# One core, blockwise FP4 feed-forward: the last group of tiles is exchanged throughout and takes its residual from a second copy of x

## The reference

```
w = weights[conditions]                      # one 64 x 64 matrix per sample
y = einsum('bct,bcd->bdt', x, w)             # mix the 64 channels of a sample
a = quant_dequant_mxfp4(y)                   # blocks of 32 along t: shared power-of-two scale,
W = quant_dequant_mxfp4(weight)              # values rounded to the FP4 grid
out = x + (a @ W.T + bias)                   # W is 512 x 512
```

## Time and profile before

| | us |
|---|---|
| runs | 97.59, 98.38, 98.47 |
| median | 98.38 |
| the profiled execution | 97.9 |
| its span, first to last instruction | 96.2 |
| PE busy / DVE busy / ACT busy | 84.4 / 81.9 / 75.3 |
| DMA moved | 22.17 MB, mean 230 GB/s |

### The profile page before, as it was taken

The page is one execution under the profiler, slowest core; times in us unless marked ns, Lnnn a source line. Parts: engine busy times, 40 slices in busy tenths (PEclk is TensorE's granted clock), DMA queues, the critical chain, the costliest instruction groups (busy, mean ns, idle before and its releaser), DMA issues.

```text
span 96.2 us, 2263 instructions
## 1 busy us (share of the span) xinstructions
PE 84.4 (88%) x715; PEld 41.2 (43%) x715; DVE 81.9 (85%) x138; ACT 75.3 (78%) x85; POOL 32.9 (34%) x60
## 2 busy tenths in 40 slices
PE   5999594999799998999899899989999989989800
PEld 4966252595482324344233433333352333445300
DVE  1248999999999999999999999999979999885600
ACT  4740498699998869999999999999999849957000
POOL 4273758399647548303000300320040021054000
PEclk9999999999999999999999999999999999999995
DMA  1898789694896789799999991896579399486992
GB/s 34 288 316 295 244 249 301 212 352 125 181 317 218 274 248 269 242 312 265 254 310 298 311 212 49 272 245 116 218 185 224 114 263 222 88 272 175 270 285 92
DMA packets 13901, 22.17 MB, mean 230 GB/s; under 512 B 4034, under 2 KB 4802, under 8 KB 13890
## 3 DMA queue, kind: packets, MB, share of 16 engines
q1 hardware_dynamic: 11456, 17.31, 56.4%
q0 software_dynamic: 2432, 4.73, 23.6%
q10 hardware_dynamic: 2, 0.00, 0.0%
HBM read 10.49 MB, written 8.39 MB: 196 GB/s over the span
## 4 chain that ended last, share of the span: by engine, by line
PE 44%; ACT 11%; DVE 10%; issue 6%; ACTq 0%; DVEq 0%
PE o_ps L357 20%; PE y_ps L357 5%; PE y_ps L306 5%; ACT y_sb L471 5%; ACT o_sb L493 4%; PE o_ps L352 4%; PE o_ps L337 3%; DVE a L654 3%; DVE n_int L625 2%; DVE top L645 2%; ACT z L463 1%; PE o_ps L382 1%; PE y_ps L367 1%; PE y_ps L300 1%; PE y_ps L318 1%
## 5 line engine op out<-in xcount | busy, mean ns | idle before, releaser
L357 PE MATMUL o_ps<-wT,aT 128*128 128x512 bf16 x100 | 23.8, 380 | 0.4 <-ACT aT L508 0.4
L183 POOL DMA_DIRECT2D mix<-in_L_cond_weights_dram x32 | 17.9, 560 | 12.4 <-issue 11.0
L625 DVE TENSOR_TENSOR n_int<-y_sb,inv 128x1024 int16<-128x1024 f32 (+1 forms) x17 | 19.5, 1155 | 0.2
L306 PE MATMUL y_ps<-x_sb,mix 64*64 64x512 f32 x120 | 15.6, 606 | 3.9 <-DMA mix<-in_L_cond_weights_dram 2.4
L272 POOL DMA_DIRECT2D x_sb<-o_sb x6 | 6.1, 1014 | 35.1 <-ACT o_sb L493 35.1
L382 PE MATMUL o_ps<-idle 128*128 128x128 bf16 x214 | 16.6, 235 | 1.2 <-DVE idle L664 1.2
L463 ACT ACTIVATE z<-y_ps 128x1024 bf16<-128x1024 bf16 x16 | 16.2, 1039 | 1.5 <-PE y_ps L306 1.2
L471 ACT COPY y_sb<-y_ps 128x1024 f32<-128x1024 f32 x16 | 16.3, 1035 | 0.0
L382 PEld LDWEIGHTS o_ps<-idle 128*128 128x128 bf16 x214 | 13.6, 105 | 5.1 <-issue 4.7
L480 ACT ACTIVATE zone<-inv 128x1024 int16<-128x1024 int16 (+2 forms) x11 | 11.6, 1074 | 3.8 <-DVE inv L618 3.8
L502 ACT COPY aT<-o_ps 128x1024 bf16<-128x1024 bf16 x14 | 13.7, 1045 | 1.0 <-PE o_ps L337 1.0
(11 more groups left out here) (52 smaller groups left out, 76.0 us busy)
## 6 DMA issues: line engine op xcount, KB each, us to landing
x_sb<-in_x_dram SPq DMA_DIRECT2D x7, 1024.0 KB, 6.4
out_dram<-x_sb SPq DMA_DIRECT2D x15, 256.0 KB, 3.6
x_sb<-o_sb POOLq DMA_DIRECT2D x6, 512.0 KB, 5.2
out_dram<-x_sb SPq DMA_DIRECT2D x6, 512.0 KB, 3.1
w_sb<-in_L_ffn_weight_dram SPq DMA_DIRECT2D x4, 256.0 KB, 3.4
x_sb<-in_x_dram SPq DMA_DIRECT2D x2, 512.0 KB, 6.6
out_dram<-x_sb POOLq DMA_DIRECT2D x4, 256.0 KB, 3.6
mix<-in_L_cond_weights_dram POOLq DMA_DIRECT2D x32, 16.0 KB, 4.5
```

Of the source, the lines that this page charges most:

```text
L183: queue.dma_start(mix[HALVES[i % 2], first + i // 2, :], table[bass.ds(row, 1), :, :].rearrange("o c d -> (o c) d")).then_inc(mix_in[step] ...
L306: last = nc.tensor.matmul(y_ps[HALVES[g], 2 * q + r, :], mix[HALVES[r], (step - 1) * GROUP + n, :], x_tiles(step, n)[HALVES[r], :], start= ...
L357: last = nc.tensor.matmul(o_bank(step, t), aT[:, t, c, :], wT[:, c, :], start=False, stop=(c == KC - 1))
L625: nc.vector.tensor_tensor(columns(n_int, t, n), columns(y_sb[:, step % 2, :, :], t, n), columns(inv, t, n), ALU.mult).then_inc(n_done, 1)
```

## The change

- The last group is mixed exchanged in both pairs (the straight form of `mix_pair` is gone), and its output tiles stay exchanged, with its transposes done one tile at a time on TensorE. Its residual therefore has to be exchanged as well: a second copy of the last group's x, `last_x`, is loaded by SP with four DMAs of 256 KB, and VectorE adds from it. The four tiles are stored by SP straight from `last_x` (three whole, the last in two halves). In DRAM such a tile is two runs of 64 rows, 256 KB apart.
- Group 7 is rescaled and turned in two pairs. Only its pair 0 gets its residual on TensorE. Tile 2 goes over `o_sb` and an accumulating DMA of POOL, tile 3 is added by VectorE. POOL takes over the store of group 6's pair 1.
- The first x is issued by ACT after its second `z_w`, not by SP ahead of the mixes. W is scaled, zoned and rounded in two pairs. TensorE's filler products (`keep_busy`) and the order of turning W and mixing group 2 move.
- `load_mixes` no longer tests the row numbers (the eight small instructions go).

Names and numbers: `after(step)` = step + 2, `late_part(part)` = 9 + part.

```diff
+        last_x = sb("last_x", [P, GROUP, T], F32)
...
+        exchanged_x_dram = x.rearrange("(s q g r) c t -> s q g r c t", q=2, g=2, r=2)
...
         def t_pair(step, q):
 
             if step < LAST - 1:
-                bank = 2 + q
-            else:
-                bank = 2 - q
-            return o_ps[:, bank, :].bitcast(BF16)
+                return o_ps[:, 2 + q, :].bitcast(BF16)
+            return y_ps[:, 3 - q, :].bitcast(BF16)
...
+                skip_runtime_bounds_check_because="cond holds row numbers of the table")
...
-            for h in range(2):
-                sp.dma_start(x_tiles(1, 2 * h, 2).rearrange("p (n t) -> p n t", n=2),
-                             x_dram[:, 2 * h:2 * h + 2, :]).then_inc(x_first_in[h], 16)
...
+            for t in range(GROUP):
+                sp.dma_start(last_x[:, t, :],
+                             exchanged_x_dram[LAST - 1, t // 2, :, t % 2, :, :]).then_inc(last_x_in, 16)
...
-                sp.wait_ge(x_added[step % 2], 16 * ((step + 1) // 2))
-                store(step, SUMMED, GROUP - SUMMED)
+                if step < LAST - 2:
+                    sp.wait_ge(x_added[step % 2], 16 * ((step + 1) // 2))
+                    store(step, SUMMED, GROUP - SUMMED)
+            sp.wait_ge(added, 1)
+            store(LAST - 1, GROUP - 1)
             for t in range(GROUP - 1):
-                sp.wait_ge(added, t + 1)
-                store(LAST, t)
+                sp.wait_ge(added, t + 2)
+                sp.dma_start(exchanged_dram[LAST - 1, t // 2, :, t % 2, :, :],
+                             last_x[:, t, :]).then_inc(stored, 16)
             for half in range(2):
-                sp.wait_ge(added, GROUP + half)
-                sp.dma_start(out_dram[:, TILES - 1, n_half(half)], x_tiles(LAST, GROUP - 1)[:, n_half(half)]
+                sp.wait_ge(added, GROUP + 1 + half)
+                sp.dma_start(exchanged_dram[LAST - 1, 1, :, 1, :, n_half(half)],
+                             last_x[:, GROUP - 1, n_half(half)]
                              ).then_inc(stored, 16)
-            sp.wait_ge(stored, 16 * (3 * (LAST - 2) + GROUP + 1))
-            sp.wait_ge(late_stored, 16 * 2 * 2)
+            sp.wait_ge(stored, 16 * (3 * (LAST - 2) - 1 + 1 + GROUP + 1))
+            sp.wait_ge(late_stored, 16 * 4)
...
+            pool.wait_ge(late_copied, 2)
+            for g in range(2):
+                pool.dma_start(exchanged_dram[LAST - 2, 0, g, :, :, :].rearrange("r c t -> c r t"),
+                               x_tiles(LAST - 1, 0, 2)[HALVES[g], :].rearrange("p (r t) -> p r t", r=2)
+                               ).then_inc(late_stored, 16)
+            pool.wait_ge(late_tile, 1)
+            pool.dma_start(x_tiles(LAST - 1, SUMMED), o_sb[:, (LAST - 1) % 2, 0, :], accum_op=ALU.add
+                           ).then_inc(x_added[(LAST - 1) % 2], 16)
+            pool.wait_ge(x_added[(LAST - 2) % 2], 16 * ((LAST - 1) // 2))
+            n0 = (LAST - 3) * GROUP + SUMMED
+            pool.dma_start(out_dram[:, n0:n0 + 2, :], x_tiles(LAST - 2, SUMMED, 2).rearrange("p (n t) -> p n t", n=2)
+                           ).then_inc(late_stored, 16)
+            pool.wait_ge(x_added[(LAST - 1) % 2], 16 * (LAST // 2))
+            n0 = (LAST - 2) * GROUP + SUMMED
+            pool.dma_start(out_dram[:, n0, :], x_tiles(LAST - 1, SUMMED)).then_inc(late_stored, 16)
...
-                if step == LAST and q == 1:
-
-                    for n in (2 * q, 2 * q + 1):
-                        for half in HALVES:
-                            last = nc.tensor.matmul(y_ps[half, n, :], mix[half, (step - 1) * GROUP + n, :],
-                                                    x_tiles(step, n)[half, :], start=True, stop=True)
-                        last.then_inc(y_ready, 1)
-                    return
...
             pe.wait_ge(y_copied, tiles_done(LAST, 3))
-            residual_pair(LAST - 1, 1)
-            for t in range(GROUP):
+            pe.wait_ge(a2_done, late_part(0))
+            turn_pair(LAST - 1, 0, straight=True)
+            residual_pair(LAST - 1, 0)
+            for t in range(2):
                 bias_tile(LAST - 1, t, start=False)
-
+            pe.wait_ge(a2_done, late_part(1))
+            turn_pair(LAST - 1, 1)
+            for t in range(2):
+                ffn_tile(LAST - 1, t)
+
+            pe.wait_ge(aT_ready, tiles_done(LAST - 1, 3))
+            for t in range(2, GROUP):
+                bias_tile(LAST - 1, t)
+            for t in range(2, GROUP):
+                ffn_tile(LAST - 1, t)
+
+            pe.wait_ge(pair_copied, 2 * (LAST - 2))
             bias_tile(LAST, 0)
...
+            def copy_late_tile():
+
+                act.wait_ge(x_added[(LAST - 1) % 2], 16 * ((LAST - 2) // 2))
+                act.wait_ge(o_ready, tiles_done(LAST - 1, SUMMED))
+                nc.scalar.copy(o_sb[:, (LAST - 1) % 2, 0, :], o_bank(LAST - 1, SUMMED)).then_inc(late_tile, 1)
...
-            for t in range(GROUP):
+            for t in range(2):
                 z_w(t)
-            zone_group(0)
+
+            for h in range(2):
+                act.dma_start(x_tiles(1, 2 * h, 2).rearrange("p (n t) -> p n t", n=2),
+                              x_dram[:, 2 * h:2 * h + 2, :]).then_inc(x_first_in[h], 16)
+            for t in range(2, GROUP):
+                z_w(t)
+            for q in range(2):
...
+            dve.wait_ge(last_x_in, 16 * GROUP)
             for t in range(GROUP - 1):
-                add_residual(LAST, t)
+                dve.wait_ge(o_ready, tiles_done(LAST, t))
+                nc.vector.tensor_tensor(last_x[:, t, :], o_bank(LAST, t), last_x[:, t, :], ALU.add).then_inc(added, 1)
             for half in range(2):
                 dve.wait_ge(o_ready, tiles_done(LAST, GROUP - 1) + half)
-                part = x_tiles(LAST, GROUP - 1)[:, n_half(half)]
-                nc.vector.tensor_tensor(part, last_half(half), part, ALU.add
-                                        ).then_inc(added, 1)
+                part = last_x[:, GROUP - 1, n_half(half)]
+                nc.vector.tensor_tensor(part, last_half(half), part, ALU.add).then_inc(added, 1)
```

More of the change, by code:

```diff
@@ L149, in tiles_done, with after, late_part @@
             return GROUP * (step - 1) + t + 1
+        def after(step):
+            return step + 2
+        def late_part(part):
+            return after(LAST - 1) + part
         def n_half(half):
@@ L180, in load_mixes @@
             _, rows = nc.values_load_multi_w_load_instructions(
-                cond_sb[:, 2 * first:2 * (first + len(tiles))], engines=[engine], min_val=0, max_val=S - 1)
+                cond_sb[:, 2 * first:2 * (first + len(tiles))], engines=[engine], min_val=0, max_val=S - 1,
+                skip_runtime_bounds_check_because="cond holds row numbers of the table")
             for i, row in enumerate(rows):
@@ L392, in _ @@
                 mix_pair(2, q)
-            pe.wait_ge(ident_ready, 1)
-            for q in range(2):
-                pe.wait_ge(a2_done, q + 1)
-                turn_pair(0, q, straight=True)
-            keep_busy(60)
+            keep_busy(48)
             mix_pair(3, 0)
-            for step in range(1, LAST):
+            for step in range(1, LAST - 1):
                 if step == 2:
@@ L415, in _ @@
                     residual_pair(step, 0)
-                pe.wait_ge(a2_done, step + 2)
+                pe.wait_ge(a2_done, after(step))
                 for q in range(2):
-                    turn_pair(step, q, straight=(q == 0 or step == LAST - 1))
+                    turn_pair(step, q, straight=(q == 0))
                 if step == 1:
@@ L459, in z_pair @@
                 if q == 0 and step > 1:
-                    act.wait_ge(z_used, step - 1)
+                    act.wait_ge(z_used, after(step - 2))
                 act.wait_ge(y_ready, tiles_done(step, 2 * q + 1))
@@ L623, in round_y @@
                 if t == 0:
[L624 removed]
+                    dve.wait_ge(inv_done, after(step))
                 nc.vector.tensor_tensor(columns(n_int, t, n), columns(y_sb[:, step % 2, :, :], t, n),
@@ new lines, in _ @@
+            other_zones(LAST - 1)
+            tree_2(LAST + 4)
+            limit(LAST - 1, after(LAST - 1), 0, 2)
+            tree_3(LAST + 4)
+            rescale(LAST - 1, late_part(0), 2 * LAST, 0, 2)
+            block_max(LAST + 2)
+            limit(LAST - 1, after(LAST - 1), 2, 2)
+            lowest_zone(LAST + 2)
+            rescale(LAST - 1, late_part(1), 2 * LAST, 2, 2)
+            lift(LAST, LAST + 2)
+            top_zone(LAST + 2)
+            invert(LAST + 2)
+            round_y(LAST, 0, 1)
@@ new lines, in _ @@
+            limit(LAST, after(LAST), 0, 1)
+            for t in range(1, GROUP):
+                round_y(LAST, t, 1)
+                rescale(LAST, late_part(1 + t), 2 * LAST + t, t - 1, 1)
+                limit(LAST, after(LAST) + t, t, 1)
+            rescale(LAST, late_part(1 + GROUP), 2 * LAST + GROUP, GROUP - 1, 1)
```

(3 more changed lines are left out.)

249 lines of the change are left out of this document (121 added, 128 removed).

## The result

| | before | changed |
|---|---|---|
| median of 4 runs, us | 98.25 | **122.48** |
| lowest and highest | 97.59, 98.47 | 122.18, 122.61 |
| span of the profiled execution | 96.2 | 120.9 |
| ratio, with its 95% interval | | **1.2476** [1.2409, 1.2543] |

The change costs 24.2 us; 118.3 was forecast, in a range of 110 to 127, and slower had a chance of 0.84. The time is inside the range, 4.2 above the forecast.

The account below looks back on a forecast made before the run. PE, DVE and ACT bound the middle in step; the last group's transfers on two engines would set the end. Lower-end span 110.2 plus 6.4 standing over gives 116.6; with 1.7 outside the span, 118.3 us, range 110 to 127.

Parts of the forecast that it names:

- Two engines: `last_x` loads and stores, first dimension 2, all run on the same 2 engines; 21.1 us for each megabyte; chance 0.81.
- The rate: Each DMA engine moves 24.8 GB/s, so the last group's 512 KB on each of two engines takes 21.1 us.
- what stands over on the two engines: Work left at 86 us from the `last_x` loads: between 0 and 12.8 us, half of it, 6.4, taken.
- an empty queue: Lower end at the last stores: nothing queues, data moves from 89.1 us, plus 21.1 gives a span of 110.2.
- other loads move forward: If other loads leave the stretch from 34 to 86 us earlier, 0 us stands over; if none does, 12.8.
- The bound of engines that never rest: Upper end: the two engines work without pause from 2.3 us on, span 119.3, or 129.7 at the slower rate.
- SP's stall: Rival: two engines, and SP's issue stalls behind full queues, delaying middle and last stores; 120 to 127; no separate chance.
- Compute: Compute ends 1.7 us earlier: 2.2 gained in the last groups, 0.5 lost at the start; last addition near 89.8.
- first maximum: Sign at the start: group 1's first maximum starts near 15.5 us, against 15.21 before.
- The 0.5 us at the start: Handling W in pairs, with ACT's two zones ahead of group 1's z: 0.5 us lost, between 1.3 gained and 1.2 lost.
- Sixteen engines: Rival: `last_x` transfers spread over all sixteen engines, last store leaves 1.7 us earlier; 96.2 us, 95 to 97.3; chance 0.13.
- POOL's chain: Rival: sixteen engines, but POOL's copy, accumulation, wait and store of group 7's tile 2 ends last; 97.5 to 98.5; chance 0.04.

Follow-up runs that it names:

- experiment 7: Kernel before, its last group's five stores given a first dimension of 2 in DRAM and issued by POOL through the software queue: 109.93 us.
- experiment 2: Changed kernel with only the loads of `last_x` split by 64 rows, the stores staying 2 x 64: 117.0 us.
- experiment 11: Kernel of experiment 10 with the start of the kernel before, the first x still issued by ACT: 97.02 us, ratio 0.9854.
- experiment 1: Changed kernel with all nine `last_x` transfers cut so that their first dimension is 64, in four loads and ten stores: 100.67 us, ratio 1.0269.
- experiments 8 and 9: 8: kernel of experiment 1, second half of each last store issued by ACT: 100.51 us. 9: additionally group 6's pair 1 stored by SP, not POOL: 99.8 us.
- Experiment 10: Kernel of experiment 9, group 7's tile 2 added by VectorE, not POOL's accumulating DMA, and stored by SP with tile 3: 97.98 us, ratio 0.9887.

## Why the prediction was right, and where it was off

**Two engines: right.** The step rested on counting packets, and each count since has come out to the unit, for first dimensions of 2, 4, 8 and 64. The Trainium skill, page "DMA: Bandwidth & Descriptors", section "Why a DMA increments its semaphore by 16 and not by 1", gives the rule that the engine count divides the slowest dimension; the counts of these hardware transfers agree with it for 2, 4 and 8. POOL's in experiment 7 can't be counted so, with sixteen closing packets for each store; its shares fit two engines for each, but not the same two.

**The rate: right.** 24.8 GB/s per engine were taken, 25.5 measured from 100 to 110 us. 1 MB at 51 GB/s is 20.6 us.

**The term that was mis-sized: what stands over on the two engines.** The prediction took half of 12.8 us, 6.4. The later of the two engines ends its data at 120.2, so its 21.1 us of stores began by the sum at 99.1, 10.0 behind the 89.1 of an empty queue: 10.0 and not 6.4. That is 3.6 of the 4.3 us by which the span is over 116.6; the other 0.7 is the time from the last data to the end, which the sum had left out. The half was argued from the idea that other loads move forward, and that they did: SP issues its last load of x at 29.08 us instead of 37.08, and the stretch before 34 us holds more than before. The kernel before and the changed one:

```profile
10.00:34.00 24.00, 20.93 (x241) 12.38 (x239) 23.34 (x37) 20.83 (x23) 16.66 (x31) 1.00 0.80 249
...
10.00:34.00 24.00, 20.49 (x242) 12.23 (x240) 22.44 (x39) 19.93 (x23) 18.05 (x34) 1.00 1.07 306
```

What the half left out went the other way. SP's loads of `last_x` and the stores behind them block SP from 32.7 to 54 us, and the stores displaced from there press on 60 to 78 us. And behind 86 us the two engines have other work besides the last stores: from 89.6 to 100 us POOL's queue moves 1.05 MB at 38.5% of sixteen engines, which is 4.0 us of each on average. How the 10.0 divides between these is not shown. The bound of engines that never rest, 119.3, was the nearer one. One can also see it from the end: in the DMA view from 100 to 118 us SP's queue moves 0.86 of the 1.05 MB, and some 0.06 follow (25 GB/s until 120.2), so in the 10 us since the first issue about an eighth had gone.

**SP's stall: a rival that happened.** It was told as an alternative of the same sign, 120 to 127, and it is in the trace: 13.04, 8.25, 12.19 us. With the loads cut (experiment 2) the first store from `last_x` is still issued at 89.26 and the end comes 4.4 us sooner, so at the end the stall is mainly the form in which the backlog shows; an extra cost of a microsecond or two isn't excluded.

**Compute: right.** Last addition 89.69 against 89.8; mixing 1.09; first maximum 15.49 against 15.5. From the start of the last group's mixing of pair 1 to the last addition it is 20.2 us instead of 22.5, 2.3 gained where the sum had 2.2, and that mixing starts 0.55 later, where it had 0.5. The 0.5 us at the start had a wrong reason, perhaps: the old start (experiment 11) doesn't bring it back. And none of it mattered, since the stores ended last.

**Sixteen engines: its price was wrong.** Had that rival come true, 95 to 97.3 would have been missed: 100.67 was measured. The sum gave the last stores the tail of before, 4.8 us, but the change also makes group 7's tile 2 a transfer of POOL's at 84.7 us that reads and writes, with a store behind it. The rival of "POOL's chain" had it as a chain with a time of its own, 97.5 to 98.5. In experiment 1 it isn't that: POOL's last store is issued at 89.94, lands 3.9 us later, and SP's stores end last; there the cost is the share that the chain takes of engines that are already full (0.94 from 90 to 92 us). In experiments 8 and 9 it is that too, by 0.7 and 0.4 us, because of POOL's closing instruction, which the rival hadn't counted. Experiment 10 takes both away and gives 1.8 us back.

## What to carry to other kernels

Before a transfer is moved or reshaped, count the closing packets of its queue: data packets taken off, they are sixteen for each transfer of SP or ACT that spreads and fewer for one that doesn't, and the first dimension tells which. (POOL's transfers have sixteen either way.) A store that is written `2 x 64 rows` for convenience costs eight times its own time on the engines, and its load the stores behind it; two DMAs of 64 rows cost one issue more. With a DMA share near 1 in the last microseconds, an addition of 0.7 us on an engine that had time was cheaper here than an accumulating DMA. And when an experiment on the tail changes nothing, see which engine is through last: another end may hide what it gave.

## What was not expected of the hardware

- A SyncE issue is not a constant: the four `last_x` loads took 0.55 to 7.9 us each, and 2.93 us together when they spread. What holds the issuer is thus what the two engines still have to do, and while it is held the DMA share is 0.41 for 9 us: the other engines run short of work.
- First dimensions of 4 and 8 cost 3.9 and 2.4 us (1.5 by the quicker run) more than the engines' time alone, of 2 a little less (17.9 against 18.5).
- The same shape from POOL's queue came with 1,792 packets of 8 or 16 bytes beside the 256 of data, used up to ten engines for five stores, and cost two thirds of SP's price.
- POOL's closing instruction lasts 6.0 to 7.8 us from its last issue on in the kernel before and in experiments 1, 8, 9 and 10, and 15.5 in experiment 7. An issue of POOL late in the kernel can so end it, after its data has landed: in experiment 8 SP is through at 97.00 and POOL at 97.70.
- The accumulating DMA landed in 9.0 us (median) in the changed kernel and 5.2 before, at the same size. It has two groups of time, so compute didn't wait for it; a kernel with less slack might have to:

```profile
x_sb<-o_sb POOLq DMA_DIRECT2D x6, 512.0 KB, 9.0
```
